# Local attention: four pairs of the second head's score tiles between the first head's, and eight value products a head on GpSimd

## The reference

```python
x = x + _L0_conv_ref(_gn(x), ...)          # window attention
x = x + _L1_conv_ref(_gn(x), w_out, b_out)

# _L1_conv_ref: p = the 25 shifted copies (zero padded), q = the pixel itself
p = patches.reshape(N, NHEADS, hdim, K2, H, W)
q = x.reshape(N, NHEADS, hdim, 1, H, W)
scores = (p * q).sum(axis=2, keepdims=True)
att = jax.nn.softmax(scores, axis=3)
out = (p * att).sum(axis=3).reshape(N, D, H, W)
out = jnp.einsum('ndhw,od->nohw', out, w_out) + b_out[None, :, None, None]
```

## Time and profile before

| | |
|---|---|
| median of 3 runs | 1668.08 us |
| the profiled execution | 1669.27 us, its span 1667.5 us |
| busy in the span | TensorE 1365.2, VectorE 1402.4, ScalarE 991.9, GpSimd 1138.1 us |
| window attention | to about 700 us |
| local attention, heads 0 to 7 | 716.38 to about 1580 us |
| last projection | about 1600 to 1667 us |

### The profile page before, as it was taken

How to read it: one execution, slowest core, us unless ns; L and a number is a source line. 1 busy time by engine, 2 the same in 40 slices (tenths; PEclk the granted TensorE clock), 3 DMA queues, 4 the chain that set the end, 5 groups by cost and what they waited for, 6 DMA issues and landing times.

```text
span 1667.5 us, 62887 instructions
## 1 busy us (share of the span) xinstructions
PE 1365.2 (82%) x26281; PEld 755.7 (45%) x26281; DVE 1402.4 (84%) x1964; ACT 991.9 (59%) x1861; POOL 1138.1 (68%) x875
## 2 busy tenths in 40 slices
PE   4889999999999999646978879798796977877664
PEld 3667777777777777412322323233232322323332
DVE  4977777777777777789999999999999998994833
ACT  3667777777777777455647567474675745562200
POOL 5445555555555555306799999999999999974700
PEclk9989999999999999876999999999999998987977
DMA  8902021202033211152024233232522323235089
GB/s 325 335 16 59 19 59 23 58 19 58 19 96 35 60 28 51 45 132 54 18 54 114 55 92 83 53 83 55 127 55 60 78 46 73 55 148 172 22 332 388
DMA packets 106870, 152.35 MB, mean 91 GB/s; under 512 B 71362, under 2 KB 83650, under 8 KB 100034
## 3 DMA queue, kind: packets, MB, share of 16 engines
q1 hardware_dynamic: 106690, 149.67, 30.9%
HBM read 77.99 MB, written 65.20 MB: 86 GB/s over the span
## 4 chain that ended last, share of the span: by engine, by line
PE 42%; POOL 21%; issue 13%; DVE 11%; ACT 9%; SPq 1%; DMA 1%; POOLq 0%; ACTq 0%; DVEq 0%
POOL arena L802 14%; PE PS L1489 8%; PE PS L1324 6%; PE PS L1350 6%; PE PS L1333 5%; POOL arena L813 5%; PE PS L1301 3%; PE PS L1433 3%; PE PS L1512 3%; PE PS L1293 2%; ACT arena L991 2%; PE PS L1464 2%; DVE arena L1197 2%; POOL arena L768 2%; DVE arena L1110 2%
## 5 line engine op out<-in xcount | busy, mean ns | idle before, releaser
L1223 DVE TENSOR_TENSOR arena<-arena,PS 128x1568 f32<-128x1568 f32 x334 | 585.1, 1779 | 20.0 <-PE PS L1489 10.7
L802 POOL TENSOR_TENSOR arena<-arena 128x1568 f32<-128x1568 f32 x168 | 516.8, 3113 | 88.8 <-PE PS L1433 68.5
L768 POOL TENSOR_TENSOR arena<-arena,consts 128x196 f32<-128x196 f32 x512 | 294.4, 610 | 301.8 <-ACT arena L852 301.8
L1489 PE MATMUL PS<-arena,consts 32*32 32x392 f32 x12800 | 400.8, 515 | 74.6 <-DVE arena L1223 21.0
L1000 ACT ACTIVATE PS<-arena 128x392 f32<-128x392 f32 x334 | 166.3, 501 | 255.1 <-DVE arena L1223 253.8
L1433 PE MATMUL PS<-arena,consts 128*32 128x392 f32 x1664 | 199.8, 552 | 85.7 <-POOL arena L802 45.5
L1489 PEld LDWEIGHTS PS<-arena,consts 32*32 32x32 f32 x12800 | 147.5, 104 | 244.9 <-issue 108.0
L877 ACT ACTIVATE arena<-PS 128x452 f32<-128x452 f32 x256 | 141.2, 552 | 144.0 <-PE PS L1333 140.6
L1350 PE MATMUL PS<-arena 128*64 128x34 f32 x4096 | 196.5, 228 | 34.9 <-POOL arena L768 21.6
L813 POOL TENSOR_TENSOR arena<-arena 128x1568 f32<-128x1568 f32 x66 | 202.1, 3074 | 31.0 <-ACT arena L940 22.4
L1350 PEld LDWEIGHTS PS<-arena 128*64 128x64 f32 x4096 | 154.9, 138 | 92.0 <-issue 32.1
(11 more groups left out here) (110 smaller groups left out, 1781.3 us busy)
## 6 DMA issues: line engine op xcount, KB each, us to landing
arena<-x_wide_dram SPq DMA_DIRECT2D x32, 660.0 KB, 8.1
arena<-x_wide_dram SPq DMA_DIRECT2D x256, 67.5 KB, 2.0
x_wide_dram<-arena SPq DMA_DIRECT2D x12, 1125.0 KB
arena<-in_x_dram SPq DMA_DIRECT2D x8, 1568.0 KB, 14.9
x_wide_dram<-arena SPq DMA_DIRECT2D x64, 196.0 KB, 4.3
x_dram<-arena SPq DMA_DIRECT2D x8, 1568.0 KB, 7.5
attn_dram<-arena SPq DMA_DIRECT2D x256, 49.0 KB, 3.0
arena<-x_dram SPq DMA_DIRECT2D x8, 1568.0 KB, 19.1
```

The source lines that it names most:

```text
L768: i = nc.gpsimd.tensor_tensor(k_bd[k][:, r], keys.unsqueeze(1).to_broadcast([P, HEADS_T, S]), head_mask.unsqueeze(2).to_broadcast([P, HEAD ...
L802: nc.gpsimd.tensor_tensor(tile, x_part, by, ALU.mult).then_inc(pool_tile, 1)
L1223: nc.vector.tensor_tensor(by_channel(v_tiles[n % V_RING]), shifted_values(half, k), over_channels(PS[:, 2 + n % W_BANKS, 0:PIX]), ALU.mult ...
L1489: mm = nc.tensor.matmul(PS[dst, 4 + i, 0:PIX], ident[src, src], tile[src, c * PIX:(c + 1) * PIX], start=done == 0, stop=done == NK - 1)
```

## The change

Three things. RING_ORDER takes a pair of head 1's score tiles ahead of the pairs 4, 6, 8 and 10 of head 0, so that GpSimd works on head 1 while VectorE works on head 0. Of each head's value products (but the last head's) GpSimd gets an eighth, number 20 of the first half, and VectorE has 42. And SyncE issues head 1's late loads at once behind head 0's, with the store of the last pair of x1 behind both. The other edits count places in the ring by the new order.

```diff
-SHARE_AT = [[8, 11, 14], [17, 19, 21, 23]]
-POOL_SHARE = [[(13, 16, 18), (13, 17, 21, 22)]] * (LH - 1) + [[range(18, NK), range(15, NK)]]
+SHARE_AT = [[8, 11, 14, 16], [17, 19, 21, 23]]
+POOL_SHARE = [[(13, 16, 18, 20), (13, 17, 21, 22)]] * (LH - 1) + [[range(18, NK), range(15, NK)]]
...
-RING_ORDER = [step for step in VECTOR_ORDER if step[0] == "score"] + [step for step in TILE_ORDER if step[0] != "scale"]
+VECTOR_SCORES = [step for step in VECTOR_ORDER if step[0] == "score"]
+SECOND_HEAD_AFTER = [4, 6, 8, 10]
+
+
+def ring_order():
+
+    order, later = [], [step for step in TILE_ORDER if step[0] != "scale"]
+    for t in range(S_TILES):
+        if t in SECOND_HEAD_AFTER:
+            order += later[:2]
+            later = later[2:]
+        order += VECTOR_SCORES[2 * t:2 * t + 2]
+    return order + later
...
-    LOADING, FIRST_LOADS = 40.0, {("s", 0): 0.0, ("s", 1): 32.0, ("v", 0): 48.0}
+    LOADING, FIRST_LOADS = 40.0, {("s", 0): 0.0, ("s", 1): 8.0, ("v", 0): 48.0}
...
-            before = ("copy", j, t - 1) if t else ("copy", j - 1, S_TILES - 1) if j else None
+            before = ("copy",) + PAIRS[PAIR_AT[j, t] - 1] if PAIR_AT[j, t] else None
...
                     for g in GROUP_ORDER[EARLY:]:
                         load_for_scores(j, a, g, xs_loaded)
-                if j == 0:
-                    store_x1(BP - 1)
-                    for a in range(2):
-                        sp.wait_ge(xs_loaded[s_buf(0, a)], 16 * EARLY * CH)
+            store_x1(BP - 1)
             sp.wait_ge(x1_stats, UNITS)
...
-                if a == 0 and (j or t):
-                    pe.wait_ge(sc_copied, j * S_TILES + t)
+                if a == 0 and PAIR_AT[j, t]:
+                    pe.wait_ge(sc_copied, PAIR_AT[j, t])
```

More of the change, by code:

```diff
@@ L156 @@
 POOL_ORDER = [step for step in TILE_ORDER if step[0] != "score" or step[2] != SQUARE]
-RING_ORDER = [step for step in VECTOR_ORDER if step[0] == "score"] + [step for step in TILE_ORDER if step[0] != "scale"]
+VECTOR_SCORES = [step for step in VECTOR_ORDER if step[0] == "score"]
[8 more added lines that the diff above has]
+    return order + later
+RING_ORDER = ring_order()
+PAIR_AT = {pair: n for n, pair in enumerate(step[1:3] for step in RING_ORDER if step[0] == "score" and step[3] == 0)}
+PAIRS = sorted(PAIR_AT, key=PAIR_AT.get)
+VECTOR_AT = {step: n for n, step in enumerate(VECTOR_SCORES)}
 SQUARE_AT = {step: n for n, step in enumerate(step for step in TILE_ORDER if step not in POOL_ORDER)}
@@ L199, in merge_orders @@
             after = [freed, ("pixels", "s", j, step[3], pieces_of("s") - 1)]
-            if n < 2 * S_TILES:
+            if j == 0:
                 add("dve", step, 0.15 + 1.04e-3 * columns, after)
@@ L505, in await_ring_tile @@
         def await_ring_tile(eng, step):
-            n = RING_AT[step]
-            if n < 2 * S_TILES:
-                eng.wait_ge(dve_score, n + 1)
+            if step in VECTOR_AT:
+                eng.wait_ge(dve_score, VECTOR_AT[step] + 1)
             elif step in SQUARE_AT:
@@ L982, in seed_max @@
             def seed_max(j):
-                act.wait_ge(sc_copied, j * S_TILES + MAX_MAPS[0][0] + 1)
+                act.wait_ge(sc_copied, PAIR_AT[j, MAX_MAPS[0][0]] + 1)
                 if j:
@@ L1200, in max_step @@
                 unit, slot = MAX_MAPS[m + 1]
-                dve.wait_ge(sc_copied, j * S_TILES + unit + 1)
+                dve.wait_ge(sc_copied, PAIR_AT[j, unit] + 1)
                 if m:
```

## The result

The changed kernel takes 1734.9 us (median of 4 runs, 1732.88 to 1738.77) against 1668.88 us of the kernel before in the same comparison (1666.13 to 1674.37). The ratio is 1.0401, 95% interval [1.0377, 1.0426]: slower, as forecast, but by 66 us where 31 were forecast, and outside the range of 1690 to 1710.

What follows compares the result with a forecast made beforehand. It took GpSimd's work, busy about 99.5 of 101 us a head, as the bound, VectorE's 97.7 close behind. Loads 6.1, score products 19.0 and heads 6.0 made +31.1 us on 1669.27: 1700.4, median 1699, range 1690 to 1710.

Steps and rivals of the forecast that it cites:

- Order of the loads: Start of local attention: the x1 store, now behind all 32 loads, delays VectorE's first score product by 6.1 us.
- Score products in turns: Head 0's preparation: each GpSimd score product holds up a VectorE one by 2.8 us, 19.0 us net.
- TensorE as the ring's bound: Rival: TensorE's sums limit the score ring, with a late store and idle kept in the heads; 1712 us, chance 0.12.
- The lead is not carried: GpSimd's lead ends at head 0's second scaling, waiting for the eviction; that scaling comes 6.9 us sooner.
- The eighth product as an amount: Heads: GpSimd has 34 products a head at 3.017 us; +9.9 us between second scalings of heads 0 and 5.
- The heads: All seven heads together: 9.9 + 3.0 - 6.9 = +6.0 us, bounds +4.9 and +11.2.
- The place of its idle is freed one VectorE value earlier in TensorE's new order: Heads: where GpSimd idled for a TensorE sum is freed 1.8 us earlier, leaving 1.1 of 6.3 us idle.
- VectorE's 97.7 becomes 96.0: Head 0: one value product fewer saves VectorE 1.7 us, with GpSimd ahead, so the period falls to 96.0 us.
- The rival of the other side: Rival: GpSimd, once ahead, is never waited for; every head runs at VectorE's 96.0 us; 1659 us, chance 0.05.

Runs made afterwards that it cites:

- e12: Kernel before, with only the planner's rank of the last totals (single sums of the softmax's denominator) put first: 1677.43 us, ratio 1.0055.
- e7: Kernel before plus only the eighth value product, GpSimd's first-half products at places 8, 10, 12, 14 of the next head's scores: 1684.47 us, ratio 1.0086.
- e2: Kernel before with only the eighth value product added, in the old ring order and with the old loads: 1716.8 us, ratio 1.028.
- e1: Changed kernel with seven value products a head as before, keeping the new ring order and loads: 1700.77 us, ratio 1.0167.
- e4: Changed kernel with GpSimd's first-half value products at places 8, 10, 12, 14 of the next head's scores, not 8, 11, 14, 16: 1705.61 us, ratio 1.0208.
- e5: Changed kernel with the eighth value product taken from the second half (number 9), not the first (number 20): 1708.24 us, ratio 1.022.
- e11: Changed kernel with the earlier product places 8, 10, 12, 14 and the last totals ranked first in the planner: 1711.47 us, ratio 1.027.
- e9: Changed kernel, with the planner told that a GpSimd value product takes 2.6 us, not 3.0, which reorders TensorE's sums: 1727.93 us, ratio 1.0345.
- e6: Changed kernel with the last totals (sums of the softmax's denominator) ranked first in the planner, not last: 1755.0 us, ratio 1.0498.
- e3: Changed kernel with the store of the last x1 pair back ahead of head 1's loads: 1727.35 us, ratio 1.0327.
- e8: Changed kernel with GpSimd's eight early score products of head 1 on half of their columns, the rest left out: 1720.56 us in one run.

## Why the prediction was wrong in size

Heads 0, and 1 to 6, in us, with what closes the first half and where 5b stands in heads 2 to 6:

| kernel | values | ring | closed at place | 5b behind | head 0 | heads 1 to 6 |
|---|---|---|---|---|---|---|
| before | 7 | old | 14 | 15 | 97.7 | 608.4 |
| e12 | 7 | old | 14 | 17 | 100.1 | 620.1 |
| e7 | 8 | old | 14 | 16 to 17 | 100.3 | 620.4 |
| e2 | 8 | old | 16 | 17 to 18 | 102.1 | 654.8 |
| e1 | 7 | new | 14 | 15 to 16 | 107.2 | 606.2 |
| e4 | 8 | new | 14 | 16 to 17 | 106.1 | 616.0 |
| e5 (product 9 of the second half) | 8 | new | 14 | 15 to 16 | 105.4 | 621.2 |
| e11 | 8 | new | 14 | 17 | 99.6 | 625.1 |
| e9 | 8 | new | 16 | 14 to 15 | 108.8 | 630.4 |
| changed | 8 | new | 16 | 17 to 18 | 108.9 | 638.4 |
| e6 | 8 | new | 16 | 19 to 20 | 101.2 | 671.2 |

- *Order of the loads: right.* Forecast +6.1, measured +5.7; the store releases VectorE, and e3 gives it back. It landed 6.7 us after issue where I took 5.8, and the issue came 14.75 us after the first load where I took 16.07.
- *Score products in turns: right in sum, 18.6 for 19.0.* GpSimd starts at 733.72 (forecast 733). The terms differ: the holds are 18.75 where I had 23.5, and TensorE's sums add 4.05, which I had put under the rival of TensorE as the ring's bound. So the sum came out partly by luck.
- *The lead is not carried: right in the wait, not in the gain.* GpSimd waits 10.37 us before the second scaling of head 0 (forecast some 7). I had a gain of 6.9 us over all heads. With the early closing the new ring gains 4.4 us in heads 1 to 6 (e4 against e7), but head 0 gives that back (106.1 against 100.3): over all seven e4 takes 722.1 us, e7 720.8. With the late closing the gain in heads 1 to 6 is 16.4 (changed against e2), in head 1 above all (101.5 against 106.8); there 5b stands behind 14 against 17, so what the lead does by itself is not shown.
- *The eighth product as an amount: right in kind where it decides, and by luck in the sum.* I had +7.7 us for heads 1 to 6 (+6.0 with -1.7 for head 0); e4 has 616.0 - 608.4 = +7.6 and its heads 2 to 6 take 103 to 104 (forecast 102 to 103). But the terms are others: from the second scaling of head 0 to that of head 5 I had +9.9, and e4 has 520.7 (911.51 to 1432.24) against 504.1, so +16.6; the rest makes up for it. Without the new ring (e7) heads 1 to 6 cost +12.0.
- *The heads: the failed step.* Forecast +6.0 (bounds +4.9 and +11.2), measured 747.3 - 706.1 = +41.2. One sentence of mine fell, and one term was missing. "The place of its idle is freed one VectorE value earlier in TensorE's new order" held for head 1 alone (5b behind 14; in head 0 behind 6); in heads 2 to 6 it stands behind 17 or 18, later than the 15 before. I carried to all heads what holds in one. And nowhere did I ask who waits for product 20: it closes the half, so its place is a term of its own, which I had at nothing. From e4 to the changed kernel heads 1 to 6 grow by 22.4 us; the two ways through the table are +14.4 (closing, to e9) then +8.0 (order), or +9.1 (order, to e11) then +13.3 (closing). So closing is about 14 and order about 8 to 9, for the corners that these orders represent: e4's order is not quite e9's, and e6's rank moves the totals too. These are no constants: in the old ring the step from e7 to e2, mostly closing, is 34.4.
- *"VectorE's 97.7 becomes 96.0" in head 0: failed.* It takes 108.9, +11.2 where -1.7 was forecast. Of this 6.5 to 7.7 go when the last total stands behind 8 value sums instead of 17 (e11 against e4; e6 with 101.2). e1 shows that it comes with the new ring, since it has 107.2 with seven products. The 3.5 us by which e6 is still over 97.7 are not settled.

Closing and order hang together, as heads 3 and 4 of the changed kernel show:

```profile
1166.00 3.04 POOL L816 TENSOR_TENSOR arena<-arena 128x1568 f32<-128x1568 f32 x1 [3.43 <-PE PS L1451]
...
1187.34 1.79 DVE L1237 TENSOR_TENSOR arena<-arena,PS 128x1568 f32<-128x1568 f32 x1 [6.46 <-PE PS L1503]
...
1269.11 2.61 DVE L1244 RECIPROCAL consts<-PS 128x392 f32<-128x392 f32 x1 [2.66 <-PE PS L1478]
...
1273.41 0.95 PE L1503 MATMUL PS<-arena,consts 32*32 32x392 f32 x32 [1.57 <-DVE arena L1237]
```

The sum of 5b lets GpSimd go on at 1166.00, its product 20 closes the half, and VectorE goes on at 1187.34. From there VectorE shows no wait until its next reciprocal (2.66 us for the last total). TensorE then waits 1.57 us for VectorE's 18th value, which stands behind that reciprocal, since it has to sum 5b of the next head after it; GpSimd goes on at 1275.37, 109.4 us after 1166.00. The period there is the length of this loop, longer than GpSimd's 102.9 us of work. By this reading, bringing product 20 or 5b forward shortens the same loop, and where it is shorter than GpSimd's work, as it seems to be in e4, the amount sets the period.

Sum: 5.7 + 18.6 + 41.2, the tail -0.4 (181.25 against 181.65), and SyncE at the loads 1.5 earlier (699.17 against 700.68; no effect of the change, since this time lies between 698.99 and 705.25 over the traces): 63.6. Of the 32.5 us between this and the forecast's 31.1, 35.2 lie in the heads.

The rival of the other side (GpSimd's lead carries all heads, 1659) fell with the scaling's wait. The rival of TensorE as the ring's bound came closest in time (1712), but its mechanism gave 4 us.

## What to carry to other kernels

When a product moves to another engine, ask first whether it is the last of an accumulation that somebody waits to close; its place then counts for more than its duration: the same eight products cost 1.021 or 1.040 by two places among GpSimd's scores. When a planner lists the queues, read its new order in every repetition of the loop, since what it did in one head was the reverse of what it did in five others. And an engine that is busy 99% of a period is not for that reason alone its bound: with one product moved from GpSimd back to VectorE, itself busy 98 of 101.5 us, and the queues listed anew, the kernel was slower too, by 0.4 and 0.6%.

## What of the hardware was not expected

Nothing in kind. In size: VectorE's pair of products beside GpSimd's takes up to 8.72 us where it takes 3.49 alone, and beside GpSimd's instructions on half the columns up to 5.19 (e8).
